# Attention units that take the values of two steps in one visit, with four tiles of probabilities and token tiles loaded twice

## The reference, cut to what matters

```python
q = (x @ wq).reshape(B, T, 32, 32); k = x @ wk; v = x @ wv      # x is layer-normed here
scores = einsum('bqhd,bkd->bhqk', q, k) / sqrt(32), causal
probs  = softmax(scores)
attn   = einsum('bhqk,bkd->bqhd', probs, v).reshape(B, T, C) @ wo
x = x + layernorm(attn)
low = einsum('bsd,hrd->bshr', layernorm(x), A)
ffn = 2 * einsum('bshr,hor,bsh->bso', low, B, 8 * softmax(router logits))
x = x + layernorm(ffn)
```

## Time and profile before

| | |
|---|---|
| median of three runs | 3328.93 us |
| the profiled execution | 3326.88 us |
| its span in the profile | 3325.1 us |
| TensorE busy | 3191.2 us, 96% |
| VectorE busy | 2163.1 us, 65% |
| GpSimd busy | 2061.2 us, 62% |
| ScalarE busy | 1661.8 us, 50% |
| DMA moved | 144.04 MB |

### The profile page before, as it was taken

The page is one execution under the profiler, slowest core; times in us unless marked ns, Lnnn a source line. Parts: engine busy times, 40 slices in busy tenths (PEclk is TensorE's granted clock), DMA queues, the critical chain, the costliest instruction groups (busy, mean ns, idle before and its releaser), DMA issues.

```text
span 3325.1 us, 45565 instructions
## 1 busy us (share of the span) xinstructions
PE 3191.2 (96%) x15976; PEld 1606.5 (48%) x15976; DVE 2163.1 (65%) x5848; ACT 1661.8 (50%) x3306; POOL 2061.2 (62%) x741
## 2 busy tenths in 40 slices
PE   7899999999999999999999999999999999999997
PEld 3444554455554455554444445544555444554444
DVE  4666677767767667774365667676776776677605
ACT  2334555555555555555433345545555554555552
POOL 1335676776676888777311176677576677778870
PEclk9999999999999999999999999999999999999998
DMA  4422111201101001101211211111010100011000
GB/s 118 116 61 65 52 52 39 61 26 30 52 23 58 23 23 30 29 23 39 64 52 52 81 45 40 42 44 60 26 56 23 39 17 23 26 43 48 7 1 26
DMA packets 133012, 144.04 MB, mean 43 GB/s; under 512 B 28200, under 2 KB 93736, under 8 KB 132784
## 3 DMA queue, kind: packets, MB, share of 16 engines
q1 hardware_dynamic: 132480, 140.72, 14.4%
q10 hardware_dynamic: 304, 0.41, 0.0%
HBM read 72.91 MB, written 16.78 MB: 27 GB/s over the span
## 4 chain that ended last, share of the span: by engine, by line
PE 73%; POOL 15%; DVE 5%; ACT 3%; issue 3%; SPq 1%; DMA 1%; POOLq 0%; ACTq 0%; DVEq 0%
PE ps L1501 14%; PE ps L1529 12%; PE ps L1490 12%; POOL ds L745 12%; PE ps L1632 11%; PE ps L1455 10%; PE ps L1542 3%; POOL ds L742 2%; PE ps L1591 2%; PE ps L1672 1%; ACT pr L842 1%; PE ps L1686 1%; PE ps L1564 1%; SPq L637 1%; PE ps L1642 1%
## 5 line engine op out<-in xcount | busy, mean ns | idle before, releaser
L842 ACT ACTIVATE pr<-ps 128x512 f32<-128x512 f32 (+3 forms) x2560 | 1299.8, 534 | 1303.0 <-PE ps L1501 885.0
L745 POOL TENSOR_TENSOR ds<-ds,pr 128x2048 f32<-128x2048 f32 (+1 forms) x360 | 1491.6, 4143 | 133.1 <-ACT pr L842 100.5
L1501 PE MATMUL ps<-qs,ks 98*128 98x512 f32 (+3 forms) x2560 | 1349.4, 534 | 22.4 <-ACT pr L842 6.7
L1095 DVE TENSOR_REDUCE mx<-ps 128x1 f32<-128x512 f32 x1536 | 1009.2, 685 | 389.7 <-PE ps L1490 381.7
L1490 PE MATMUL ps<-ks,qs 96*128 96x512 f32 (+3 forms) x2560 | 957.2, 385 | 51.6 <-ACT pr L842 28.8
L1501 PEld LDWEIGHTS ps<-qs,ks 98*128 98x128 f32 x2560 | 482.9, 190 | 763.7 <-issue 294.6
L1092 DVE CUSTOM_DVE_ANT_0 ps<-ps,mask_qk 128x128 f32<-128x128 f32 (+3 forms) x1024 | 498.4, 503 | 476.5 <-PE ps L1490 471.6
L1490 PEld LDWEIGHTS ps<-ks,qs 96*128 96x128 f32 x2560 | 486.7, 192 | 312.3 <-ACT pr L842 157.6
L1529 PE MATMUL ps<-pr,vs 128*32 128x512 f32 (+3 forms) x5120 | 612.0, 546 | 0.6 <-POOL pr L752 0.3
L1455 PE MATMUL ps<-xT,wq_sb 128*128 128x512 f32 x1024 | 513.7, 599 | 5.5 <-ACT zs L885 3.1
L1632 PE MATMUL ps<-wo_sb,ao 128*128 128x512 f32 x896 | 453.4, 598 | 0.5 <-DVE q L1084 0.5
(11 more groups left out here) (166 smaller groups left out, 2105.7 us busy)
## 6 DMA issues: line engine op xcount, KB each, us to landing
qs<-q SPq DMA_DIRECT2D x762, 64.0 KB, 2.0
wq_sb<-in_L_attn_wq_dram SPq DMA_DIRECT2D x64, 512.0 KB, 4.0
t<-in_L_attn_x_dram SPq DMA_DIRECT2D x32, 512.0 KB, 6.3
xr<-in_L_attn_x_dram SPq DMA_DIRECT2D x28, 512.0 KB, 4.6
out_dram<-xr SPq DMA_DIRECT2D x28, 512.0 KB, 4.7
wo_sb<-in_L_attn_wo_dram SPq DMA_DIRECT2D x8, 512.0 KB, 5.2
qs<-mT SPq DMA_DIRECT2D x252, 4.0 KB
xT<-in_L_attn_x_dram SPq DMA_DIRECT2D x4, 512.0 KB, 5.5
```

Of the source, the lines that this page charges most:

```text
L745: nc.gpsimd.tensor_tensor(ds[:, :, c0:], ds[:, :, c0:], this, ALU.add).then_inc(added, 1)
L842: nc.scalar.activation(pr[:, k % NS, g, c0:], ps[:, PM + EXP_PLACE[head(n, t, g)] % NPM, c0:], ACT.Exp, scale=SCALE).then_inc(exp_done, 1)
L1095: nc.vector.tensor_reduce(found, seen, AX.X, ALU.max).then_inc(mx_done, 1)
L1501: last = nc.tensor.matmul(ps[:, bank, c0:], ks[0:STK + 2, c:c + P], qs[0:STK + 2, n % NS, g, c0:], start=True, stop=not by_mask)
```

## The change: two steps of values in one visit

It has three parts.

1. In the long blocks (more than 16 slots), the units with u from 1 to 4 are `paired`: after an even step nothing is visited, and after the odd step that follows the values of both are done, one behind the other, with the sums of both where TensorE has them.
2. `pr` gets a fourth tile (`NPR = 4`): step k now waits for the values and the add of step k - 4. `NS = 3` stays for the query tiles.
3. The room comes from `t4`, which has two tiles instead of four. Tokens 0 and 1 are loaded for their statistics, then 2 and 3 into the same tiles, then 0 and 1 again for norm (POOL) and transpose, then 2 and 3 again, whose norm is now done by ACT in halves. The transposes of tokens 0 and 1 move from the start of unit 5 to slots 44 to 53 of unit 4 (in short blocks they stay near the end of unit 4). In the last block the tiles that t4 no longer has are those of wq (`tail_t`), and for block 0 those of xr.

The diff, cut to its core:

```diff
+    NPR = 4
@@ values_at
-        if n_ < 0:
+        if n_ < 0 or paired(n_) and t_ % 2 == 0:
             return []
         after = 1 if not zeroed(n_, t_) else 2 if t_ == steps(n_) - 1 else 3
-        return [(n_, t_)] if g == after else []
+        if g != after:
+            return []
+        return [(n_, t_ - 1), (n_, t_)] if paired(n_) else [(n_, t_)]
+
+    def paired(n):
+        return slots(n) > 16 and n % NU in (1, 2, 3, 4)
...
-    TURN_AT = (64 * 5, 3)
+    TURN_AT = (64 * 4 + 44, 3)
+    BACK = (20, 14)
@@ enter
-        at(28 if blk == 1 else 4, "SP", "tokens", blk)
+        back = BACK[N == 16]
+        for i in range(2):
+            at(28 if blk == 1 else 4, "SP", "tokens", blk, i, False)
         for i in range(TB):
             t0 = 64 + 48 * i if blk == 1 else 64 * i + 42
+            at(t0 + 8, "SP", "tokens", blk, (i + 2) % TB, i >= 2)
...
-            at(64 * 4 + 4 + 8 * i if N == 16 else 64 * i + 64 + NORM_AT, "POOL", "norm", blk, i)
+            if i < 2:
+                at(64 * 4 + 4 + 8 * i if N == 16 else 64 * i + 64 * 3 + NORM_AT, "POOL", "norm", blk, i)
+            else:
+                at(T0 + apart * (2 * i - 2) - 1, "SP", "tokens", blk, i, True)
+                for h in range(2):
+                    at(T0 + back + apart * (2 * i + h) - 4, "ACT", "norm", blk, i, h)
             for h, who in enumerate(("ACT", "DVE")):
-                at(T0 + apart * (2 * i + h), "PE", "tr", blk, i, h)
-                at(T0 + apart * (2 * i + h), who, "tr", blk, i)
+                first = T0 + apart * (2 * i + h) + (back if i >= 2 else 0)
+                at(first, "PE", "tr", blk, i, h)
+                at(first, who, "tr", blk, i)
@@ tiles
-        t4 = sb("t4", [P, TB, D])
+        t4 = sb("t4", [P, 2, D])
-        pr = sb("pr", [P, NS, GH, BLK])
+        pr = sb("pr", [P, NPR, GH, BLK])
@@ ScalarE, exps
-                if g == 0 and k >= NS:
-                    act.wait_ge(pv_done, k - NS + 1)
-                    if by_gpsimd(*step_of(k - NS)):
-                        act.wait_ge(added, adds_to(*step_of(k - NS)))
+                if g == 0 and k >= NPR:
+                    act.wait_ge(pv_done, k - NPR + 1)
+                    if by_gpsimd(*step_of(k - NPR)):
+                        act.wait_ge(added, adds_to(*step_of(k - NPR)))
@@ ScalarE, new
+            def token_norm(blk, i, h):
+                act.wait_ge(x_loaded[i], 16 * (2 * blk + 1))
+                act.wait_ge(nb_ready, (blk - 1) * TB + i + 1)
+                half = t4[:, i % 2, h * HALF:(h + 1) * HALF]
+                nc.scalar.activation(half, half, ACT.Identity, scale=LN["pre"]["r"][:, i:i + 1],
+                                     bias=nb[:, i:i + 1]).then_inc(xn_act, 1)
@@ SyncE, load_tokens
+                if blk and again and i >= 2:
+                    sp.wait_ge(xt_ready, 2 * (TB * blk + i - 2) + 2)
+                elif blk and (again or i >= 2):
+                    sp.wait_ge(LN["pre"]["s_st"], 2 * (TB * blk + (i + 2) % TB) + 2)
+                elif blk:
+                    sp.wait_ge(xt_ready, 2 * (TB * (blk - 1) + i + 2) + 2)
+                sp.dma_start(tokens(blk, i), x_t[blk * TB + i]).then_inc(x_loaded[i], 16)
```

More of the change, by code:

```diff
@@ L424, in bass_mqa_sandwich_lora_router @@
         xn_ready = sem("xn_ready")
+        xn_act = sem("xn_act")
         xt_ready = sem("xt_ready")
@@ L530, in bass_mqa_sandwich_lora_router, with tokens, tail_t @@
         x0n_dve = sem("x0n_dve")
+        def tokens(blk, i):
+            return xr[:, i - 2, :] if blk == 0 and i >= 2 else t4[:, i % 2, :]
+        def tail_t(i):
+            return wq_sb[:, i - 2, :, :].rearrange("p k c -> p (k c)") if i >= 2 else t4[:, i, :]
         def kv_of(blk):
@@ L618, in _, with load_tokens @@
         def _(sp):
-            def load_tokens(blk):
-                for i in range(TB):
-                    if blk:
-                        sp.wait_ge(xt_ready, 2 * TB * blk)
-                    sp.dma_start(t4[:, i, :], x_t[blk * TB + i]).then_inc(x_loaded[i], 16)
+            def load_tokens(blk, i, again):
+                if blk and again and i >= 2:
[5 more added lines that the diff above has]
+                sp.dma_start(tokens(blk, i), x_t[blk * TB + i]).then_inc(x_loaded[i], 16)
             def load_wq(n):
@@ L663, in ffn_weights @@
                                  fb_v[n]).then_inc(wt_loaded, 16)
-            load_tokens(0)
+            for i in range(TB):
+                load_tokens(0, i, False)
             load_wq(0)
@@ L734, in add @@
                     pool.wait_ge(masked, masks_to(n, t))
-                this = pr[:, (UNIT_STEP[n] + t) % NS, :, c0:]
+                this = pr[:, (UNIT_STEP[n] + t) % NPR, :, c0:]
                 if t == 1:
-                    first = pr[:, UNIT_STEP[n] % NS, :, :]
+                    first = pr[:, UNIT_STEP[n] % NPR, :, :]
                     if n:
@@ L750, in mask @@
                 pool.wait_ge(exp_done, head(n, t) + GH)
-                here = pr[:, (UNIT_STEP[n] + t) % NS, :, c0:c0 + P]
+                here = pr[:, (UNIT_STEP[n] + t) % NPR, :, c0:c0 + P]
                 nc.gpsimd.affine_select(out=here, in_=here, compare_op=ALU.is_ge, fill=0.0, base=0,
@@ L793, in _ @@
                     pool.wait_ge(t_scaled, 2 * i + h + 1)
-                    nc.gpsimd.tensor_tensor(x4[:, i, half], x4[:, i, half], t4[:, i, half], ALU.add).then_inc(t_out_pool, 1)
+                    nc.gpsimd.tensor_tensor(x4[:, i, half], x4[:, i, half], tail_t(i)[:, half], ALU.add).then_inc(t_out_pool, 1)
         @block.scalar
@@ L803, in first_norm @@
                 act.wait_ge(head_nb, 1)
-                nc.scalar.activation(t4[:, i, :], t4[:, i, :], ACT.Identity, scale=LN["pre"]["r"][:, i:i + 1],
+                nc.scalar.activation(tokens(0, i), tokens(0, i), ACT.Identity, scale=LN["pre"]["r"][:, i:i + 1],
                                      bias=nb[:, i:i + 1]).then_inc(x0n_act, 1)
@@ L949, in _ @@
                             turned(*a)
+                        elif stage == "norm":
+                            token_norm(*a)
                         elif stage == "proj":
@@ L1394, in tail_out @@
                     dve.wait_ge(t_scaled, 2 * i + h + 1)
-                    nc.vector.tensor_tensor(x4[:, i, half], x4[:, i, half], t4[:, i, half], ALU.add).then_inc(t_out_dve, 1)
+                    nc.vector.tensor_tensor(x4[:, i, half], x4[:, i, half], tail_t(i)[:, half], ALU.add).then_inc(t_out_dve, 1)
             for c in range(TB):
@@ L1529, in values @@
                     last = nc.tensor.matmul(ps[g * HD:(g + 1) * HD, PPV, c0:], vs[:, row, :],
-                                            pr[:, (UNIT_STEP[n] + t) % NS, g, c0:], start=(t == 0), stop=(t == steps(n) - 1))
+                                            pr[:, (UNIT_STEP[n] + t) % NPR, g, c0:], start=(t == 0), stop=(t == steps(n) - 1))
                 if whole(n) and t == 0:
@@ L1570, in turn @@
                 if blk:
-                    pe.wait_ge(xn_ready, j + 1 - TB)
+                    if i < 2:
+                        pe.wait_ge(xn_ready, 2 * (blk - 1) + i + 1)
+                    else:
+                        pe.wait_ge(xn_act, 4 * (blk - 1) + 2 * (i - 2) + h + 1)
                     if (j, h) in TR_PLACE:
@@ L1579, in turn @@
                     kk = h * KT // 2 + k
-                    last = nc.tensor.transpose(ps[:, turn_bank(j, h), k * P:(k + 1) * P], t4[:, i, kk * P:(kk + 1) * P], ident[:, :])
+                    last = nc.tensor.transpose(ps[:, turn_bank(j, h), k * P:(k + 1) * P], tokens(blk, i)[:, kk * P:(kk + 1) * P], ident[:, :])
                 last.then_inc(xt_ready, 1)
@@ L1752, in tail_begin @@
                 pe.wait_ge(early_sb, 2 * TB if tail_bank(i, h) == PX else 2 * i + h + 1)
-                nc.tensor.matmul(ps[:, tail_bank(i, h), :], ident[:, :], t4[:, i, h * HALF:(h + 1) * HALF], start=True, stop=False)
+                nc.tensor.matmul(ps[:, tail_bank(i, h), :], ident[:, :], tail_t(i)[:, h * HALF:(h + 1) * HALF], start=True, stop=False)
                 for k in range(EARLY, KT - 1):
```

26 lines of the change are left out of this document (15 added, 11 removed).

## The result

The changed kernel takes 3308.42 us, the median of five runs (3300.21 to 3315.59), against 3328.93: 0.9937 of the time before (95% interval 0.9923 to 0.9951), 20.5 us less, where 44.6 us were forecast. It lies inside the wide range of 3258 to 3312 and outside the sum's own, 3270 to 3297. The profiled execution is the median one: 3308.42 us with a span of 3306.7.

What follows compares the result with a forecast made beforehand. TensorE was taken as the bound, POOL setting the pace in places. Merges -43.2, mask waits +5.6, ACT +3, fourth tile -10 and tokens 0 sum to -44.6 us: about 3284 us, own range 3270 to 3297, wide range 3258 to 3312.

Steps and rivals of the forecast that it cites:

- pairs, with their two waits: Paired units of long blocks: merged visits -43.2 us, late masks +5.6 us, ACT's exponentials +3 us.
- Merges, 144 x 0.30: TensorE in paired units: two visits made one save 0.30 us, 144 times, -43.2 us (26 to 50).
- ACT cannot keep up, +3: Steps without a visit run faster than ACT's four exponentials: 0.12 us once per each of 24 units, +3 us (0 to 10).
- Diagonal masks, +5.6: 16-step paired units: TensorE waits for POOL's mask of step 13, 1.3 us in two units, 0.5 in six.
- Fourth tile, -10: Exponentials wait less for POOL's adds, but masks still stand behind those adds: -10 us (0 to -20).
- Tokens, 0: Norms moved from POOL to half-idle ACT, transposes to unit 4: 0 us, at worst 22.6 lost, at best 6 gained.
- The clock: A sign of being wrong: granted clock below 1.00 in units 11, 19 and 27; no size given.
- The range: The sum's own 3270 to 3297, 14 us a side: tile 10, ACT 5, merges 7, added as squares.
- rivals: 1: Everything comes through: no mask is late and the fourth tile gives 19 us, so 3267 us; chance 0.13.
- Rival 2: POOL bounds 16-step units, the tile gives nothing: 3305 us; late reloads, 7 blocks x 3 us, end there too; chance 0.12.
- Rival 3: Going out and in for a visit costs TensorE nothing by itself, so merges save nothing: 3324 us; chance 0.07.
- rival 4: Slower: at the first diagonal pair TensorE waits 3.4 us for a mask in each of 24 units, 3360 us; chance 0.06.

Runs made afterwards that it cites:

- at half width: The changed kernel with VectorE's maxima reading only the first half of each score tile's keys: 3281.13 us with pairs, 3307.61 us without.
- the pairs alone: The kernel before with only the paired visits added, three tiles of probabilities and tokens as before: 3332.34 us.

## Why the forecast of 44.6 us was wrong, and what of it held

**The sum, term by term**, at equal clock:

| term | forecast | measured |
|---|---|---|
| tokens | 0 (-6 to +22.6) | +11.4 |
| fourth tile | -10 (-20 to 0) | -16.8 |
| pairs, with their two waits | -34.6 | -23.2 |
| lower granted clock | not in the sum | up to +7.8 |
| all | -44.6 | -20.8 (means) |

Two steps failed: the tokens at 0, and the +3 for ACT's exponentials in a slot without a visit. Against the forecast the tokens took 11.4 us, the pairs 11.4 and the clock, for which there was no term, up to 7.8; the tile gave 6.8 back.

- **Merges, 144 x 0.30: right in price.** 0.31 us in the trace of a plain visit, and 2.21 us for the eight of unit 27 with VectorE lightened. That the pairs then give 34.4 us in all, as the -34.6 of the sum, is chance: the 10 us below 44.6 are not the two waits forecast.
- **ACT cannot keep up, +3: failed.** The doubt was the right one, put mostly on the wrong engine and in the wrong size. I compared TensorE's shorter slot with ACT's 0.6 us exponential. In each slot stands also a maximum of 0.68 us on VectorE, beside its small operations; the earlier trace rows had VectorE at 54.84 of 75 us, above ACT's 42.05. It costs 11 us, shown by the two widths of maxima with and without pairs. ACT has a share after all, by its copy of the output projection and not by the four exponentials: 5.4 us in the 12-step units.
- **Diagonal masks, +5.6: wrong in kind.** I let all groups of the visit wait for both masks, and the section on the change says so too. Only the values of 13 need mask 13, and they come 1.74 us behind those of 12. TensorE also came to the pair 2 us later than I had it (68.4 us after the unit's start, not 66.3): 1.1 of them go to VectorE (67.2 at half width), and 0.9 are the values and sums of step 14 of unit 26, which moved into slot 2 of unit 27 and which I had left out. In the 16-step units of u = 1 to 4 a mask holds a weight load for 0.3 us at a time, 0.6 in a unit at most. The diagonal pairs do gain little, and in unit 27 that is for VectorE's reason.
- **Fourth tile, -10: right in mechanism, low in size.** ACT's waits for adds in L777 fell from 155.3 to 37.2 us, and the masks behind those adds did hold TensorE, for 20.2 us. What I had not seen is that the pairs live on it. I wrote that the merge would be given back without it; in the 16-step units more than all of it is.
- **Tokens, 0: failed.** It is +11.4. "TensorE's work is the same" was true, and no argument: the transposes went from a unit with gaps to one without, and where they left they had covered a wait. The norms on ACT, which I hid wholly, make 4 of it. The late reload, for which I allowed "a us or two", holds ACT for 0.6 us.
- **The clock** stood among the signs only. The earlier trace rows has it at 0.95 and 0.97 in the two units with more than 0.3 us of idle time, so a doubt was to be had, but no price: unit 16 of the kernel before idles for 2.5 us at 1.00, and the pairs alone raise TensorE's idle time from 133.9 to 162.3 us without a lower clock.
- **The range.** Its last part, a fifth of the merges, is 8.6 and not 7; with 8.6 the root of the squares is the 14 that stands there.

Against the rivals: 1 is excluded by the median of 3308. Rival 2 forecast 3305 by POOL's bound; the number is near, the mechanism is not, for unit 27 takes 72.80 us at half width with the same POOL time (59.63 us) as in 74.27. Its other half, 3 us per block for a late reload, is not there: ACT waits once for it, 0.6 us. Rival 3 is excluded by the double visit, rival 4 by the short waits for masks.

Open: what makes the clock fall sooner in one run than in another. The waits that precede it are shown, not what decides. Open too are some 5 us of the pairs, and where the 2 us of the diagonal pairs outside their units lie.

## What to carry to other kernels

When work is taken off the busiest engine, compare the shortened stretch with every engine that has a fixed price per stretch, the one with the highest busy share first; and ask what the removed piece had been covering. Where a resource is freed by moving other work, price the move by the place it goes to (has it gaps?) and the place it leaves (what waits there next?), not by the work. Take a change of several parts apart before it is kept: here one part cost what another gave, and two were worth something only together.
